# A gated attention and mixture-of-experts block on one core: ramp and attention order rebuilt, GpSimd's early splits done step by step, fewer float32 products in the FFN

## The chip, the cores and the metric
The kernel runs on 1 core of one Trainium2 chip. The metric is device time in microseconds (us) of one execution; lower is better. Engines are named as in the profile: PE is TensorE's matmuls, PEld its weight loads, DVE VectorE, ACT ScalarE, POOL GpSimd, SP the engine that issues the DMAs.

## The reference
Two batches of 256 tokens with 128 features, and 512 context rows each.

```
x = x + tanh(g_xattn) * (attention(layernorm(x), ctx) @ Wo + bo)     # 8 heads of 64; keys and values
                                                                    # from 512 context rows and 256 own rows
x = x + tanh(g_ffn) * ffn(layernorm(x))
ffn(x): logits = x @ gate_w + gate_b; top 2 of 8 experts, softmax over the two
        out = sum_e combine[e] * (gelu(x @ w1[e] + b1[e]) @ w2[e] + b2[e])   # all 8 experts are computed
        + gelu(x @ ws1 + bs1) @ ws2 + bs2                                    # shared expert
```

## The kernel before
**Precision.** Most products are computed from float16 pairs. A float32 operand is scaled and written as a high half (hi) and a low half (lo), and `three` runs hi*hi, hi*lo and lo*hi into the same PSUM bank: three matmuls for one product. The second products of the FFN named in `FULL32` (experts 0 to 8 of batch 0, and the last product, number 17) read float32 operands directly instead, from the loaded weights in `ring` and the gelu output in `hid`.

**Ramp.** `x` and the context are loaded, the rows of x are normalised (statistics on DVE, the power on POOL), both are transposed on PE and split into hi (ACT) and lo (DVE). The items in `PRE` (context transposes `tc`, x transposes `tx`, keys of pair 0, queries of pair 0) come first. `split_a` splits Wk2, Wk1 and Wq: ACT writes the hi half, DVE the lo half.

**Attention.** A pair is two heads of one batch; there are 8 pairs, and each is cut into 3 units of 256 keys, so 24 steps (units), numbered 0 to 23. In step i, PE computes the scores of unit i (`scores`), the weighted values of an earlier pair (`values`, one head in each of two of every three steps), a chunk of the row maxima of the pair after the current one (`max_chunk`), and the projections listed in `LATE[i]`. ACT takes the exponential (`exp_unit`, L640), writes its hi half (`make_hi`, L648) and evicts the projections (L629). POOL computes the lo half of the probabilities (`prob_lo`, L541), and may be at most 3 units behind, since `prob` has 3 buffers. DVE reduces the maxima (`part_max`, L821), evicts the lo halves of the projections (L803) and normalises a pair of heads (`normalise`, L850). Until unit `DOUBLE0` the scores have one PSUM buffer: the scores of unit i+1 start after the exponential of unit i.

**Tail of a batch.** `tail` transposes the output of attention (O0, O1), multiplies by Wo (WO, with a bias row as two more matmuls), adds to x, normalises again (X) and computes the gates (GATE, COMB, B2). `TAIL_STEP` gives the step of each.

**FFN.** Steps from `FFN0` = 24. Product k (0 to 17; 9 per batch) has its first matmuls at step 24+k, gelu on ACT in the same step (L711), its second matmuls two steps later and the addition to `acc` on DVE (L971) three steps later. For a product not in `FULL32` the gelu output is split: DVE and ACT write a half of hi each (L935, L719), POOL the lo half (L561). The expert weights are split once, during batch 0: the hi half by ACT (L723, L728) or POOL (`early_hi` L503, `late_hi` L530), the lo half by DVE (`expert_lo`, L925), for expert 0 by POOL (`early_lo`, L515).

The order on each engine is that of its loop over the steps, written out by hand: an engine that waits holds all that stands behind it.

Of the kernel before, what the change touches and what calls it, by code (L numbers as in the profile page):

```python
# [13 lines left out]
F32 = mybir.dt.float32  # L14
# [25 lines left out]
RING = 7  # L40
# [20 lines left out]
DOUBLE0 = 15  # L61
# [8 lines left out]
EARLY_HI_STEP = (14, 17, 20)  # L70
EARLY_LO_STEP = (16, 19, 22)
WO_STEP = 12

W1_STEP = {4: FFN0, 5: FFN0 + 1, 6: FFN0 + 3, 7: FFN0 + 5, 8: FFN0 + 6}
# [3 lines left out]
W1_LATE, W2_LATE, W2P_LATE = list(W1_STEP), list(W2_STEP), list(W2P_STEP)  # L78
# [25 lines left out]
def values_of(s):  # L104
# [7 lines left out]
PRE = [(("tc", 0), 0), (("tx", 0), 2), (("k", 0, 0), 4), (("q", 0), 6)]  # L112
LATE = {
# [20 lines left out]
WARM_START, WARM_LAYERNORM, WARM_MAX, WARM_STEP = 14, 9, 4, 12  # L134
# [55 lines left out]
FULL32 = [*range(NE), NF - 1]  # L190
# [27 lines left out]
def block_kernel(nc, x, ctx_in, g_xattn, g_ffn, Wq1, Wk1, Wv1, Wk2, Wv2, Wo, bo,  # L218
                 gate_w, gate_b, w1, b1, w2, b2, ws1, bs1, ws2, bs2, out):
    stack = ExitStack()  # L220
    with stack:
# [12 lines left out]
        wa = sb("wa", [P, 2, NW, 512], F16)  # L234
# [12 lines left out]
        oT = qo  # L247
# [21 lines left out]
        bo_row = sb("bo_row", [1, D], F32)  # L269
        unit_row = sb("unit_row", [1, P], F32)  # L270
# [1059 lines left out]
```

## Time and profile before

| | |
|---|---|
| median of 3 runs | 158.71 us (158.71 to 159.02) |
| profiled execution, its own time | 158.72 us |
| its span in the trace | 156.9 us |
| mean granted TensorE clock | 0.999 |

The span is what the trace shows from the first instruction to the last, so 1.8 us of the execution's time lie outside of it. The times inside the trace are from the span's start.

### The profile page before, as it was taken

The page shows a single profiled execution, that of the slowest core. Times are in us where ns is not written, and L with a number is a line of the kernel's source. Part 1 is how long each engine was busy: PE and PEld are TensorE (multiplying, and loading weights), DVE is VectorE, ACT ScalarE, POOL GpSimd, SP SyncE. Part 2 cuts the span into 40 slices and gives each one's busy share as a digit, 9 for nine tenths or more (in the row PEclk, how much of TensorE's full clock was granted, in tenths as well). Part 3 has the DMA queues.
Part 4 walks back from the last instruction along what each step waited for, and adds up shares of the span by engine and source line. Part 5 has one row for each costly group of instructions (what it writes and reads, how often), then busy time and mean ns, then how long its engine had stood idle before and what let it go on. Part 6 is the DMA issues. An engine that isn't in the chain of part 4 may idle for free.

```text
span 156.9 us, 4455 instructions
## 1 busy us (share of the span) xinstructions
PE 143.6 (92%) x1844; PEld 110.4 (70%) x1844; DVE 107.6 (69%) x204; ACT 116.6 (74%) x196; POOL 97.6 (62%) x84
## 2 busy tenths in 40 slices
PE   7969699999899998986989789999999999999992
PEld 4624354466466565755767579999999999989992
DVE  1679898977867787769786565426674677597731
ACT  3546789998887889997657989875458576978730
POOL 5504988596555676999698988400260079688730
PEclk9999999999999999999999999999999999999999
DMA  5589880000000000400000000054000000100001
GB/s 151 183 295 265 266 255 0 0 4 2 4 0 6 0 4 0 117 23 0 4 0 4 4 0 4 0 148 123 0 0 6 0 2 0 38 0 4 0 4 33
DMA packets 10112, 7.66 MB, mean 49 GB/s; under 512 B 1086, under 2 KB 8300, under 8 KB 10092
## 3 DMA queue, kind: packets, MB, share of 16 engines
q1 hardware_dynamic: 10092, 7.38, 15.7%
q8 instruction: 15, 0.25, 0.7%
q14 instruction: 5, 0.04, 0.1%
HBM read 7.11 MB, written 0.26 MB: 47 GB/s over the span
## 4 chain that ended last, share of the span: by engine, by line
PE 67%; DVE 14%; ACT 9%; issue 5%; DMA 2%; POOL 1%; DVEq 0%; ACTq 0%
PE banks L1286 11%; PE banks L1000 11%; PE banks L1002 10%; PE banks L1001 10%; DVE part L821 6%; ACT prob L640 4%; PE banks L1179 3%; PE banks L1181 3%; PE banks L1180 3%; PE banks L1129 2%; ACT v_hi L629 2%; DMA x_sb<-in_x_dram 2%; PE banks L1147 2%; ACT p_hi L648 2%; PE banks L1139 2%
## 5 line engine op out<-in xcount | busy, mean ns | idle before, releaser
L541 POOL TENSOR_TENSOR p_lo<-prob,p_hi 128x1024 f16<-128x1024 f32 x23 | 49.3, 2150 | 14.9 <-ACT p_hi L648 14.9
L711 ACT ACTIVATE prob<-banks,b1T 128x256 f32<-128x256 f32 x72 | 28.1, 474 | 11.1 <-PE banks L1002 11.1
L821 DVE TENSOR_REDUCE part<-banks 128x2 f32<-128x1024 f32 (+1 forms) x24 | 29.0, 1215 | 1.6 <-PE banks L1102 1.5
L640 ACT ACTIVATE prob<-banks 128x1024 f32<-128x1024 f32 x24 | 24.5, 1021 | 6.9 <-PE banks L1147 6.8
L648 ACT ACTIVATE p_hi<-prob 128x1024 f16<-128x1024 f32 x24 | 25.4, 1057 | 0.8
L1000 PE MATMUL banks<-x2h,wf 128*128 128x256 f16 x72 | 19.6, 273 | 0.0
L1286 PE MATMUL banks<-ring,prob 128*128 128x128 f32 x160 | 19.6, 276 | 0.0
L1002 PE MATMUL banks<-x2h,wf 128*128 128x256 f16 x72 | 19.6, 273 | 0.0
L1001 PE MATMUL banks<-x2h,wf 128*128 128x256 f16 x72 | 19.6, 272 | 0.0
L561 POOL TENSOR_TENSOR k_both<-prob,k_both 128x1024 f16<-128x1024 f32 x8 | 17.1, 2132 | 4.1 <-ACT k_both L719 3.0
L1179 PEld LDWEIGHTS banks<-v_hi,p_hi 128*128 128x128 f16 x192 | 17.4, 98 | 2.8 <-issue 2.7
L1179 PE MATMUL banks<-v_hi,p_hi 128*128 128x65 f16 x192 | 19.2, 195 | 0.0
L1180 PE MATMUL banks<-v_lo,p_hi 128*128 128x64 f16 x192 | 19.1, 193 | 0.0
L1181 PE MATMUL banks<-v_hi,p_lo 128*128 128x65 f16 x192 | 19.0, 194 | 0.0
L1286 PEld LDWEIGHTS banks<-ring,prob 128*128 128x128 f32 x160 | 18.7, 192 | 0.1
L1180 PEld LDWEIGHTS banks<-v_lo,p_hi 128*128 128x128 f16 x192 | 17.5, 98 | 0.0
L1181 PEld LDWEIGHTS banks<-v_hi,p_lo 128*128 128x128 f16 x192 | 17.6, 97 | 0.0
L925 DVE SCALAR_TENSOR_TENSOR wf<-ring,wf 128x512 f16<-128x512 f32 x16 | 15.6, 996 | 1.1 <-ACT wf L723 1.1
L935 DVE CAST k_both<-prob 128x512 f16<-128x512 f32 x8 | 10.3, 1283 | 5.6 <-ACT prob L711 5.6
L1000 PE MATMUL banks<-wf,k_both 128*128 128x128 f16 x64 | 11.1, 219 | 0.1
L1002 PE MATMUL banks<-wf,k_both 128*128 128x128 f16 x64 | 11.1, 219 | 0.0
L1001 PE MATMUL banks<-wf,k_both 128*128 128x128 f16 x64 | 11.1, 219 | 0.0
(158 smaller groups left out, 331.5 us busy)
## 6 DMA issues: line engine op xcount, KB each, us to landing
ring<-in_L_ffn_w_dram SPq DMA_DIRECT2D x16, 256.0 KB, 4.1
wf<-in_ctx_dram SPq DMA_DIRECT2D x2, 256.0 KB, 5.2
ring<-in_L_xattn_Wk_dram SPq DMA_DIRECT2D x2, 256.0 KB, 4.4
ring<-in_L_xattn_Wv_dram SPq DMA_DIRECT2D x2, 256.0 KB, 7.4
ring<-in_L_ffn_ws_dram SPq DMA_DIRECT2D x2, 256.0 KB, 6.8
x_sb<-in_x_dram SPq DMA_DIRECT2D x1, 256.0 KB, 2.9
ring<-in_L_xattn_Wq_dram SPq DMA_DIRECT2D x1, 256.0 KB, 4.6
ring<-in_L_xattn_Wo_dram SPq DMA_DIRECT2D x1, 256.0 KB, 8.0
```

The source lines that it names most:

```text
L541: nc.gpsimd.tensor_tensor(p_lo[:, u % RINGP, :, :].rearrange("p a n -> p (a n)"), prob[:, u % RINGE, :], p_hi[:, u % RINGP, :, :].rearrang ...
L640: nc.scalar.activation(prob[:, u % RINGE, :], units(u).rearrange("p a n -> p (a n)"), ACT.Exp, scale=DH ** -0.5 / S_SCORE).then_inc(exp_do ...
L648: nc.scalar.activation(p_hi[:, u % RINGP, :, :].rearrange("p a n -> p (a n)"), prob[:, u % RINGE, :], ACT.Copy).then_inc(ph_act, 1)
L711: nc.scalar.activation(hid[:, k % NHID, c * T1:(c + 1) * T1], span(2 * (k % 2), HC * T1)[:, c * T1:(c + 1) * T1], ACT.Gelu, bias=b1T[:, e ...
L821: nc.vector.tensor_reduce(dst, src, AX_X, ALU.max).then_inc(part_done, 1)
L1000: nc.tensor.matmul(dst, w[0], a[0], start=start, stop=False)
L1001: nc.tensor.matmul(dst, w[0], a[1], start=False, stop=False)
L1002: return nc.tensor.matmul(dst, w[1], a[0], start=False, stop=stop)
L1179: nc.tensor.matmul(o_ps[:, half, q, :], ph, vh, start=(t == 0), stop=False, skip_group_check=True)
L1180: nc.tensor.matmul(o_ps[:, half, q, 0:DH], ph, vl, start=False, stop=False, skip_group_check=True)
L1181: last = nc.tensor.matmul(o_ps[:, half, q, :], pl, vh, start=False, stop=(t == KT - 1), skip_group_check=True)
L1286: last = nc.tensor.matmul(banks[:, 4 + k % 2, q * D:(q + 1) * D], hid[:, k % NHID, at:at + P], ring_f(k % NE)[:, 1, cols], start=(c == 0), ...
```

## The change
1. **Ramp.** x is loaded in two halves. Only batch 0's rows are normalised, transposed and split in the ramp; batch 1's statistics are taken at step 4, its power at step 5 on POOL (six small operations, four of them new), its rows are written by ACT at step 5, and its transposes become an item at step 6. ACT and DVE split the three weights after both transposes. Keys and queries of pair 0 have their own semaphores: ACT evicts hi and a scaled float32 copy (`raw0`), DVE the queries' hi, POOL subtracts for the lo halves. `open_scores(0)` runs the first twelve matmuls of unit 0 ahead of its shift; `close_scores` adds the last four.
2. **Attention order.** Queries are computed per batch (`q0`, `q1`) instead of for both; `LATE` is spread anew, out to step 16; `DOUBLE0` goes from 15 to 18. In the ramp, the lo halves of pair 1's keys and queries stand ahead of pair 1's maxima on DVE, and at step 0 PE takes the items ahead of the chunk. Values are normalised one head at a time in one shared region of bank 6.
3. **GpSimd.** The splits of expert weights 0 to 3 run at steps 1, 3 and 5 (expert 0) and at the nine steps of `EARLY_STEP`: hi, scaled and lo all on POOL. DVE's three `expert_lo` for them are gone. W2 of experts 5, 6 and 7 is split wholly by POOL at steps 25, 26 and 27.
4. **Output projection.** Wo is no longer split: its product reads float32, without the bias matmuls; POOL adds tanh(g)*bo to x beforehand. The transposed attention output is one DVE copy instead of ACT hi and DVE lo.
5. **FFN.** `FULL32` loses products 4 to 7. Products 0 and 1 have their first matmuls together at step 24. The last product's second half is in bank 7 with its own semaphore. `RING` goes from 7 to 8.

```diff
-RING = 7
+RING = 8
-DOUBLE0 = 15
+DOUBLE0 = 18
-EARLY_HI_STEP = (14, 17, 20)
-EARLY_LO_STEP = (16, 19, 22)
-WO_STEP = 12
+EARLY_STEP = (6, 7, 9, 10, 12, 13, 15, 16, 17)
+POOL_W2 = (5, 6, 7)
+POOL_W2_STEP = (FFN0 + 1, FFN0 + 2, FFN0 + 3)
-W2_STEP = {1: FFN0 + 2, 2: FFN0 + 4, 3: FFN0 + 7, 4: FFN0 + 8}
-W2P_STEP = {5: FFN0 + 4, 6: FFN0 + 5, 7: FFN0 + 6, 8: FFN0 + 8}
+W2_STEP = {4: FFN0 + 2, 1: FFN0 + 6, 2: FFN0 + 7, 3: FFN0 + 8}
-TAIL_STEP = [dict(zip(TAIL_STAGES, (16, 17, 19, 22, 23, 28, 29))),
+TAIL_STEP = [dict(zip(TAIL_STAGES, (16, 17, 18, 21, 23, 28, 29))),
+NORM_STEP = [20, 31]
-PRE = [(("tc", 0), 0), (("tx", 0), 2), (("k", 0, 0), 4), (("q", 0), 6)]
+PRE = [(("tc", 0), 0), (("tx", 0), 2)]
+K0_BANK, Q0_BANK = 4, 7
 LATE = {
     -3: [(("k", 0, 1), 4)],
-    -2: [(("q", 1), 7)],
-    0: [(("k", 0, 2), 4), (("q", 2), 7)],
-    1: [(("v", 0, 0), 4), (("v", 0, 1), 5), (("v", 0, 2), 7)],
-    2: [(("v", 0, 3), 4), (("v", 0, 4), 5)],
-    3: [(("v", 0, 5), 7)],
-    4: [(("k", 0, 3), 4), (("q", 3), 7)],
+    -2: [(("q0", 1), 7)],
+    0: [(("k", 0, 2), 4), (("q0", 2), 7)],
+    1: [(("v", 0, 0), 4), (("v", 0, 1), 5)],
+    2: [(("v", 0, 2), 7), (("v", 0, 3), 4)],
+    3: [(("v", 0, 4), 5), (("v", 0, 5), 7)],
+    4: [(("k", 0, 3), 4), (("q0", 3), 7)],
     5: [(("tc", 1), 7)],
-    6: [(("k", 1, 0), 4)],
-    7: [(("v", 1, 0), 4), (("v", 1, 1), 5), (("v", 1, 2), 7)],
...
+    6: [(("tx", 1), 4), (("v", 1, 0), 7)],
+    7: [(("k", 1, 0), 4), (("q1", 0), 7)],
+    8: [(("q1", 2), 7)],
...
+    16: [(("k", 1, 3), 4)],
 }
-WARM_START, WARM_LAYERNORM, WARM_MAX, WARM_STEP = 14, 9, 4, 12
+WARM_START, WARM_LAYERNORM, WARM_KEYS, WARM_MAX, WARM_STEP = 14, 4, 8, 3, 8
-FULL32 = [*range(NE), NF - 1]
+FULL32 = [*range(POOL_W2[0] - 1), NE - 1, NF - 1]
-        o_ps = banks[:, 6, 0:2 * QT * (DH + 1)].rearrange("p (h q d) -> p h q d", h=2, q=QT)
+        o_ps = banks[:, 6, 0:QT * (DH + 1)].rearrange("p (q d) -> p q d", q=QT)
...
             for i in range(CHUNK0, STEPS):
+                if 0 < i < NU:
+                    open_scores(i)
                 if 0 <= i < NU:
-                    scores(i)
+                    close_scores(i)
...
```

New functions on POOL and ACT, with what they issue:

```
def second_by_pool(j):      # three 128x512 operations: hi = src*S_W; src = src*S_W; lo = src - hi
def add_bias():             # bo*tanh(g), then four 128x128 additions to x
def second_rows():          # ACT: two 128x128 rows of batch 1, scaled and shifted
```

## Rows read from the trace of the kernel before

**Rows 1.** The page's table of busy time: us, share of span, instructions.
```profile
PE 143.6 (92%) x1844; PEld 110.4 (70%) x1844; DVE 107.6 (69%) x204; ACT 116.6 (74%) x196; POOL 97.6 (62%) x84
```

**Rows 2.** The chain that ended last, in the ramp: start, us, what.
```profile
3.63 0.88 DVE stats L754 x4
...
6.29 1.22 DVE xn L772 x4
...
12.49 3.50 DVE part L821 x3
...
16.26 0.61 DVE qo L803
17.00 0.31 PE banks L1112
...
18.89 0.88 DVE k_both L803
```

**Rows 3.** Timeline of ACT: start, duration, of exponentials 0, 1, 6 and 23.
```profile
18.54 1.02 ACT L640 ACTIVATE prob<-banks 128x1024 f32<-128x1024 f32 x1 [1.10 <-PE banks L1147]
...
22.63 1.02 ACT L640 ACTIVATE prob<-banks 128x1024 f32<-128x1024 f32 x1 [0.33 <-PE banks L1147]
...
37.68 1.02 ACT L640 ACTIVATE prob<-banks 128x1024 f32<-128x1024 f32 x1 [0.35 <-PE banks L1147]
...
90.67 1.01 ACT L640 ACTIVATE prob<-banks 128x1024 f32<-128x1024 f32 x1
```

**Rows 4.** Windows: stretch, its us, busy PE, PEld, DVE, ACT, POOL, clock, DMA.
```profile
28.00:38.00 10.00, 9.69 (x139) 6.03 (x136) 8.62 (x12) 9.56 (x14) 7.47 (x4) 1.00 0.01 2
...
100.00:110.00 10.00, 10.00 (x98) 9.46 (x97) 4.93 (x11) 6.68 (x16) 0.00 (x0) 1.00 0.39 107
```

**Rows 5.** Groups of instructions: busy us, mean ns of one, idle before them.
```profile
L541 POOL TENSOR_TENSOR p_lo<-prob,p_hi 128x1024 f16<-128x1024 f32 x23 | 49.3, 2150 | 14.9 <-ACT p_hi L648 14.9
...
L925 DVE SCALAR_TENSOR_TENSOR wf<-ring,wf 128x512 f16<-128x512 f32 x16 | 15.6, 996 | 1.1 <-ACT wf L723 1.1
...
L935 DVE CAST k_both<-prob 128x512 f16<-128x512 f32 x8 | 10.3, 1283 | 5.6 <-ACT prob L711 5.6
...
L629 ACT ACTIVATE v_hi<-banks 128x512 f16<-128x512 f32 x12 | 6.5, 589 | 0.2 <-PE banks L1002 0.2
...
L530 POOL TENSOR_TENSOR wf<-ring,c_sw 128x512 f16<-128x512 f32 x4 | 4.1, 1039 | 0.0
```

**Rows 6.** Timeline of DVE around step 16: start, duration.
```profile
71.48 2.47 DVE L925 SCALAR_TENSOR_TENSOR wf<-ring,wf 128x512 f16<-128x512 f32 x1
...
100.23 0.68 DVE L925 SCALAR_TENSOR_TENSOR wf<-ring,wf 128x512 f16<-128x512 f32 x1
```

**Rows 7.** Timeline of PE: matmuls that it waited for.
```profile
74.61 0.66 PE L1190 MATMUL banks<-ident,o_sb 128*128 128x128 f32 x4 [1.28 <-DVE qo L855]
...
88.65 0.41 PE L1207 MATMUL banks<-ident,xn 128*128 128x128 f32 x2 [0.89 <-ACT xn L655]
...
91.81 0.39 PE L1212 MATMUL banks<-gw,x2T 128*128 128x8 f32 x2 [0.59 <-DVE x2h L855]
```

**Rows 8.** Timeline of PE in the FFN: starts of work, one after the other.
```profile
108.62 0.22 PE L1000 MATMUL banks<-wa,qo 128*128 128x128 f16 x1
...
110.99 0.28 PE L1000 MATMUL banks<-x2h,wf 128*128 128x256 f16 x1
...
112.31 1.95 PE L1286 MATMUL banks<-ring,prob 128*128 128x128 f32 x16
```

**Rows 9.** The same view, product 10's second matmuls and what follows.
```profile
134.87 0.22 PE L1000 MATMUL banks<-wf,k_both 128*128 128x128 f16 x1
...
136.21 0.38 PE L1218 MATMUL banks<-ident,comb 128*9 128x128 f32 x2
```

**Rows 10.** The chain that ended last, in the FFN and at the end.
```profile
122.73 1.79 PE banks L1286 x16
...
154.13 0.35 DVE acc L971
```

More of the change, by code:

```diff
@@ L404, in item_out @@
             kind = ITEMS[n][0]
-            return span(BANK[n], KEYS) if kind == "k" else banks[:, BANK[n], :]
+            if kind == "k":
+                return span(BANK[n], KEYS)
+            return banks[:, BANK[n], 0:T1] if kind in ("tx", "q0") else banks[:, BANK[n], :]
+        raw0 = prob[:, RINGE - 1, :]
+        k0_out = span(K0_BANK, KEYS)
+        q0_out = banks[:, Q0_BANK, 0:T1]
+        k0_rows = [k_nat[:, hl, 0, 0, :] for hl in range(2)]
+        q0_rows = [q_nat[:, hl, 0, 0, :] for hl in range(2)]
         block = stack.enter_context(nc.Block())
@@ L688, in _ @@
                     exp_unit(i)
+                for b in range(B):
+                    if i == NORM_STEP[b]:
+                        normal_rows(b)
+                if 0 <= i < NU:
                     make_hi(i)
+                if i == NORM1_STEP:
+                    second_rows()
                 for n in late_items(i):
@@ L1032, in item_of @@
                 if kind == "tx":
-                    keep_warm(WARM_LAYERNORM, 6)
-                    for t in range(NT):
-                        pe.wait_ge(xn_ready, t + 1)
-                        last = nc.tensor.transpose(dst[:, t * P:(t + 1) * P], xn[:, t, :], ident[:, :])
+                    b = item[1]
+                    if b == 0:
+                        keep_warm(WARM_LAYERNORM, 6)
+                    for t in range(QT):
+                        pe.wait_ge(xn_ready, QT * b + t + 1)
+                        last = nc.tensor.transpose(dst[:, t * P:(t + 1) * P], xn[:, QT * b + t, :], ident[:, :])
                 elif kind == "tc":
@@ L1112, in shift_row, with score_tiles, open_scores @@
                 nc.tensor.transpose(shift_ps_rows, nmax[:, p % 2, :], ident[:, :]).then_inc(shift_ps, 1)
-            def scores(u):
+            def score_tiles(u):
+                p, third = divmod(u, UPP)
+                return [(n, half, slice(n * T1, (n + 1) * T1),
+                         slice((KT2 * third + n) * P, (KT2 * third + n + 1) * P))
+                        for n in range(KT2) for half in range(2)]
+            def open_scores(u):
                 p, third = divmod(u, UPP)
@@ L1144, in scores @@
                     pe.wait_ge(shift_done, p + 1)
-                for n, half, cols, keys in tiles:
+                for n, half, cols, keys in score_tiles(u):
                     rows = slice(DH * half, DH * half + DH)
@@ L1225, in tail, with first_matmul @@
                 last.then_inc(misc_ps, 1)
+            def first_matmul(k):
+                b, e = k // NE, EORDER[k % NE]
+                if k == 0:
+                    pe.wait_ge(part_done, UPP * NPAIR)
+                if k == 1:
+                    pe.wait_ge(exp_done, NU)
+                if k >= 2:
+                    pe.wait_ge(gelu_done, HC * (k - 1))
+                if k == 0:
+                    pe.wait_ge(e_lo, 1)
+                elif k < EARLY:
+                    pe.wait_ge(e_lo, k + 1)
+                elif k < NE:
+                    pe.wait_ge(w1_lo, k - EARLY + 1)
+                if k % NE == 0:
+                    pe.wait_ge(misc_done, MISC[(TAIL_X, b)] + 1)
+                tok = slice(b * T1, (b + 1) * T1)
+                for c in range(HC):
+                    cols = slice(c * P, (c + 1) * P)
+                    last = three(span(2 * (k % 2), HC * T1)[:, c * T1:(c + 1) * T1],
+                                 (wf[:, 0, e, 0, cols], wf[:, 1, e, 0, cols]),
+                                 (x2h[:, 0, tok], x2h[:, 1, tok]))
+                    if c % 2 == 1:
+                        last.then_inc(h_ps, 1)
@@ L1285, in _ @@
                             if k in FULL32:
[L1286 removed]
+                                last = nc.tensor.matmul(banks[:, y_bank(k, q), q * D:(q + 1) * D],
                                                         hid[:, k % NHID, at:at + P], ring_f(k % NE)[:, 1, cols],
```

377 lines of the change are left out of this document (212 added, 165 removed), and 12 rows, old and new, of the table LATE.

## The prediction

> **What bounds the kernel now.** I read the page's busy table first, then the chain that ended last, then PE's timeline for the places where it waited, and last the windows and groups of the engines that could take PE's place. PE is busy for 92% of the span, far ahead of ACT, DVE and POOL [rows 1]. A busy PE is not a PE at its peak, so I asked in each stretch what the next piece of work waits for.
>
> The exponentials mark the stretches [rows 3]: the ramp ends at 18.54 us, step 1 starts at 22.63, step 6 at 37.68, step 23 at 90.67.
> - Ramp (0 to 18.5): a serial chain. DVE's statistics, its four row normalisations, three maxima in a row of 3.50 us, then a low half of the queries (0.61) that has to leave bank 6 before the transpose of the shift may start at 17.00 [rows 2].
> - Steps 1 to 5 (22.6 to 37.7): ACT. In 28 to 38 it is busy for 9.56 of 10 us [rows 4]. With one score buffer every step needs an exponential, its high half and that step's evictions on ACT.
> - Steps 6 to 23: PE, with holes where it waits for DVE or ACT: 1.28 and 0.89 us are two of them [rows 7].
> - FFN (from 92): PE alone. In 100 to 110 it is busy for all of 10 us, while POOL has nothing to do [rows 4]. There a matmul saved is time saved.
>
> **The change part by part.**
>
> *Ramp.* Two tiles instead of four in the statistics and the normalisation save half of 0.88 and half of 1.22 us [rows 2]: 1.05. The rest is order: x's low half, the first queries and their evictions have 256 columns instead of 512, and ACT's weight splits now stand behind x's eviction, so that part is given back. I take 1.9 us earlier for the first maximum (12.49 to 10.6); the bounds are 1.0 (the halved work alone, all reordering worth nothing) and 2.6. The three maxima, 3.50 us, stay. The low half of 0.61 us ahead of the shift's transpose goes, since no item uses bank 6 any more: 0.6. Twelve of unit 0's sixteen matmuls are done before the shift; they lie in the 1.54 us between the transpose at 17.00 and the exponential at 18.54 [rows 2, 3], of which I take 0.3. That puts the first exponential 2.8 us earlier, at 15.7. What could be late next is POOL: it must subtract 768 and 256 columns for the first low halves, priced by its 2.15 us for 1024 columns [rows 5], so 2.2 us, within the 3.5 us of maxima: hidden. The granted clock is 1.00 in all the windows shown [rows 4]; 37 instead of 39 warming matmuls should leave it so.
>
> From exponential 0 to 1 it is 4.09 us now [rows 3]. There the low halves of pair 1 wait behind a maximum (the chain has 0.88 us for the keys' at 18.89 [rows 2]) and PE's next projection waits for them. With the halves first, the maximum (about 1.2 us, a third of 3.50) comes later, and the chunk behind it. Both are needed before scores 1, so only the overlap with PE's 1.3 us of projections is won; I take 0.3. Bounds: 0.9 gained, 0.3 lost. Exponential 1: 3.1 us earlier.
>
> *Steps 1 to 5.* ACT stays the bound. It gets two row normalisations for batch 1 and loses half of two query evictions and has one value eviction moved out of step 1 and back into step 3. By 0.59 us for 512 columns [rows 5] this is about +0.3 us in 15.05. POOL gets the two 1024-column passes of expert 0 that lay in the ramp (4.0 at 2.15 each, a little less).
>
> *Steps 6 to 23.* DVE's `expert_lo` at 71.48 takes 2.47 us, where the same operation takes 0.68 at 100.23, with POOL idle [rows 4, 6]. Behind it in DVE's queue stands the low half of the attention output, and PE waits 1.28 us for that [rows 7]. The change takes this and its two like out of DVE's queue and makes the eviction one copy: 1.28 gone. Batch 0's second normalisation comes two steps earlier, which removes the 0.89 at 88.65 (the rows) [rows 7]. Wo's product took from 108.62 to 110.99 for batch 1 [rows 8], 2.37 us; as eight float32 matmuls it should cost what a second product does, 1.79 [rows 10]: 0.58 less, here once. Against this, PE gets the queries of batch 1, which lay in ACT's stretch: two items of six 256-column matmuls, at 12 such in 1.32 us [rows 8], so 1.3, and two transposes, 0.2. Sum: -1.28 - 0.89 - 0.58 + 1.5 = -1.25. The even spread of values and keys is worth nothing in this sum, because a step lasts as long as PE's work in it; it fills steps 14 to 16, which are short now. Bounds: -2.9 (the moved work falls into holes) and +2.0 (see POOL below).
>
> The Trainium skill, "SBUF — State Buffer", Who interferes with whom, says that a DVE instruction with two SBUF inputs and a GpSimd instruction that reads SBUF exclude each other for the whole instruction, and whichever started first holds the port. Here the trace agrees: 2.47 against 0.68 us on L925. The rule speaks against part of this change too: see the third rival.
>
> *POOL.* By step 17 it has extra: two expert 0 passes (4.0), batch 1's power (1.4, an estimate: no row shown has these small operations; bounded by 0 and by one pass of 2.15), three `scaled` and three `lo` at 1.04 each (6.2), less Wo's low half (1.0): about 10.6 us. Its idle time ahead of `prob_lo` is 14.9 us in all [rows 5]. It fits, with 4 us to spare, and `prob` lets POOL be up to three units behind. I take nothing for it.
>
> *FFN start.* PE waits 0.59 us for x's low half before the gates [rows 7]; with the transposes a step earlier this is hidden: -0.6. Bounds: 0 and 1.0.
>
> *FFN.* A float32 second product takes 1.79 us [rows 10], a split one 1.34 (134.87 to 136.21 [rows 9]): 0.45 less, for four products 1.8. Wo for batch 1: 0.58. At the end one of the two additions of 0.35 us [rows 10] runs beside PE's last half: 0.35. Sum: -2.7. The cover for what the splits cost elsewhere: POOL gets nine operations of 1.04 (9.4 us) at steps 25 to 27 and four low halves of 2.15; it is idle from 100 to 110 now [rows 4]. ACT gets four conversions of half a gelu output, 512 columns each, bounded by its 0.59 for an eviction of that size [rows 5]. DVE gets four casts (1.28 mean, 10.3 us in 8 [rows 5]), which it does now for batch 1 in the same rhythm. But in batch 0 it also has the weights' low halves, so I give 0.6 back. Bounds: 0 and 3.0 (all the gain of this part).
>
> **Sum.** -3.1 + 0.3 - 1.25 - 0.6 - 2.7 + 0.6 = -6.75 us. The profiled execution took 158.72 us (span 156.9), practically the median of 158.71. So 158.7 - 6.8 = 151.9 us.
>
> **The rivals.**
> 1. *POOL binds in attention.* For: at the new pace the first `prob_lo` starts near 18, and until step 17 POOL has 17 times 2.15 plus 14 us to do, some 51 us, where the steps give it about 54. If a few of its operations run late, as small ones do, each late one holds an exponential three units on. Against: three units of slack. Price: half of the 4 us to spare is missed and 2.5 us are added: 154.4. The waits of ACT would show `<-POOL p_lo` in steps 7 to 17.
> 2. *The ramp's gain isn't kept.* The ramp runs ahead, but steps 1 to 5 are ACT's and gain nothing, and step 0 to 1 gets longer because the chunk now stands behind the projections and behind two low halves and a maximum. Price: the step gets 1.5 us longer instead of 0.3 shorter: 153.7.
> 3. *DVE binds in batch 0's FFN.* Steps 29 to 33 give it a cast, two additions (0.7) and a weight's low half each. With POOL busy, casts take 1.28 in the mean and `expert_lo` up to 2.47 [rows 5, 6]: 4.4 us against PE's 2.65 to 3.1. Four steps at 1 us more than PE, less the 0.6 that I gave: 155.3. Against: the sixteen L925 have a mean of only 1.0, and casts hide well for batch 1. By the skill's rule named above, the wait ends with POOL's operation, so it should be at most one operation each time.
> 4. *Slower.* Values are normalised one head at a time in one region: the second head's matmuls must wait for DVE's normalisation of the first, which stands behind evictions and a shift. It happens once per pair, eight times. It decides if it costs over 0.9 us each time; at 1.0 us it adds 8 us: 159.9. For: DVE held PE for 1.28 us in such a manner [rows 7]. Against: a full step (about 3 us) lies between the two heads, and DVE loses three operations of up to 2.47.
> 5. *The parts do more than I give.* The moved queries fall into holes (-1.5) and the lock costs nothing (-0.6): 149.8.
>
> **How the numbers follow.** Chances: the forecast (150.5 to 153.3) 0.56, rival 1 0.10, rival 2 0.11, rival 3 0.08, rival 5 0.07, slower by rival 4 0.05, a gain eaten up to nothing by a mixture 0.03. The range reaches from rival 5 to rival 3: 149.7 to 155.4, leaving out less than 2 in 10. A measurement of this kernel tells about 0.2% (0.3 us) from no change, so: faster 0.92, same 0.02, slower 0.06.
>
> **What would show each step.** The first maximum near 10.6 and exponential 0 near 15.7 (ramp); exponential 1 near 19.5; exponential 6 near 34.9; exponential 23 near 86.6; no PE wait above 1 us in front of the transposes of the output; no PE wait in front of the gates, which now start 1.14 us behind exponential 23 (90.67 to 91.81); from there to the end about 2.7 us less. Split second products of 4 to 7 take 1.34 us each with no hole before them. It would be wrong if ACT waits for POOL's `p_lo`, if PE waits for DVE's normalisation before values, if DVE is over 90% busy in steps 28 to 33, or if the clock falls below 1.00 in the ramp.

## The result, and the profile after

The changed kernel takes 150.46 us (median of 6 runs, 149.81 to 151.60), the kernel before 158.71 us beside it. The ratio is 0.9486, with a 95% interval of 0.9447 to 0.9526. The forecast was 151.9 us. The profiled execution took 151.20 us with a span of 149.4 us; before it was 158.72 and 156.9 us, so the two spans differ by 7.5 us. The profiled execution is 0.7 us slower than the median, so the stretches below explain 7.5 us and not the 8.25 us between the medians. In the table of the experiments the slowest run of e7 (152.94 us) and that of e10 (151.09 us) were in a slower state, and the ratios leave them out.

The first view is again the page's busy table (us, share of the span, instructions), answering to [rows 1].

```profile
PE 141.4 (95%) x1862; PEld 110.2 (74%) x1862; DVE 105.4 (71%) x217; ACT 116.7 (78%) x199; POOL 120.4 (81%) x108
```

PE has only 2.2 us less to do, but the span is 7.5 us shorter: most of the gain is time in which PE waited. POOL has 23 us more to do. ACT's timeline gives the same four exponentials as [rows 3]: 0, 1, 6 and 23.

```profile
16.99 1.02 ACT L709 ACTIVATE prob<-banks 128x1024 f32<-128x1024 f32 x1 [0.46 <-PE banks L1254]
...
20.10 1.02 ACT L709 ACTIVATE prob<-banks 128x1024 f32<-128x1024 f32 x1
...
36.05 1.01 ACT L709 ACTIVATE prob<-banks 128x1024 f32<-128x1024 f32 x1
...
86.59 1.00 ACT L709 ACTIVATE prob<-banks 128x1024 f32<-128x1024 f32 x1
```

With the four of before they cut the 7.5 us into stretches:

| stretch | before | after | difference | forecast |
|---|---|---|---|---|
| start to exponential 0 | 18.54 | 16.99 | -1.55 | -2.8 |
| exponential 0 to 1 | 4.09 | 3.11 | -0.98 | -0.3 |
| 1 to 6 | 15.05 | 15.95 | +0.90 | +0.3 |
| 6 to 23 | 52.99 | 50.54 | -2.45 | -1.25 |
| 23 to the end of the span | 66.23 | 62.81 | -3.42 | -2.7 |
| sum | 156.9 | 149.4 | -7.50 | -6.75 |

The chain that ended last shows where this profiled ramp lost time (start, us, what; it answers to [rows 2]).

```profile
1.20 3.67 DMA wf<-in_ctx_dram
5.01 1.09 PE banks L1124 x4
...
8.35 1.91 DVE wa L851 x3
```

The chain no longer begins with x's landing and DVE's statistics but with the landing of context 0. The windows (stretch, us, then busy PE, PEld, DVE, ACT, POOL, clock, DMA) answer to [rows 4], with one more stretch in which POOL is full.

```profile
28.00:38.00 10.00, 9.38 (x148) 6.53 (x147) 8.83 (x19) 9.90 (x14) 9.02 (x9) 1.00 0.01 3
45.00:56.00 11.00, 11.00 (x193) 7.42 (x189) 8.39 (x15) 9.59 (x12) 11.00 (x7) 1.00 0.01 3
...
100.00:110.00 10.00, 10.00 (x90) 9.36 (x89) 8.11 (x19) 5.44 (x13) 8.87 (x10) 1.00 0.01 2
```

ACT still bounds steps 1 to 5 (9.90 of 10). In the FFN, POOL is now busy for 8.87 us of 10 where it had nothing to do, and PE has all of 10 as before. The groups (busy us, mean ns of one, idle before them) answer to [rows 5].

```profile
L586 POOL TENSOR_TENSOR p_lo<-prob,p_hi 128x1024 f16<-128x1024 f32 x23 | 48.9, 2134 | 1.1 <-ACT p_hi L717 1.0
...
L1013 DVE CAST k_both<-prob 128x512 f16<-128x512 f32 x12 | 13.0, 1081 | 5.6 <-ACT prob L784 5.6
...
L1003 DVE SCALAR_TENSOR_TENSOR wf<-ring,wf 128x512 f16<-128x512 f32 x9 | 9.7, 1077 | 0.4 <-ACT wf L801 0.3
```

POOL's idle time before the probabilities' low halves fell from 14.9 to 1.1 us, while DVE's casts got cheaper (1.08 instead of 1.28 us). PE's timeline, for the matmuls that [rows 7] showed waiting:

```profile
67.36 0.39 PE L1071 MATMUL banks<-cT,wa 128*128 128x512 f16 x1 [0.22 <-DVE v_lo L878]
...
85.72 0.61 PE L1316 MATMUL banks<-gw,x2T 128*128 128x8 f32 x4
86.18 0.27 PE L1071 MATMUL banks<-x2h,wf 128*128 128x256 f16 x1
...
90.81 0.20 PE L1286 MATMUL banks<-v_hi,p_hi 128*128 128x65 f16 x1 [0.59 <-DVE o_sb L928]
...
117.57 0.61 PE L1316 MATMUL banks<-gw,x2T 128*128 128x8 f32 x4 [0.15 <-DVE x2h L933]
```

The waits of 1.28, 0.89 and 0.59 us are gone. The gates start 0.87 us ahead of exponential 23 instead of 1.14 behind it. One new wait of 0.59 us is that of the values behind head 14's normalisation.

How full PE is from exponential 6 to the first FFN matmul is read from two more windows, the first of before (37.68 to 92.28), the second of after (36.05 to 86.18):

```profile
37.68:92.28 54.60, 49.10 (x832) 34.36 (x831) 40.27 (x60) 45.87 (x53) 43.24 (x26) 1.00 0.04 12
```
```profile
36.05:86.18 50.13, 49.79 (x833) 35.74 (x830) 36.92 (x72) 42.70 (x51) 48.45 (x32) 1.00 0.01 2
```

PE was idle for 5.50 us of this stretch and is idle for 0.34. The three waits of [rows 7] are 2.76 us of it. The other 2.7 us are four waits that neither [rows 7] nor the prediction has. Two of them, in PE's timeline of before (the wait for a maximum, `part`, comes again at 69.71 and 79.31):

```profile
42.14 0.39 PE L1000 MATMUL banks<-wa,cT 128*128 128x512 f16 x1 [0.69 <-DVE k_both L803]
...
61.57 0.39 PE L1102 MATMUL banks<-k_both,qo 64*128 64x256 f16 x4 [0.67 <-DVE part L821]
```

The same view for Wo's product and a split second product, answering to [rows 8] and [rows 9] (each lasts until the next start shown):

```profile
103.46 1.95 PE L1306 MATMUL banks<-wo,k_both 128*128 128x128 f32 x16
105.24 0.27 PE L1071 MATMUL banks<-x2h,wf 128*128 128x256 f16 x1
...
110.39 0.22 PE L1071 MATMUL banks<-wf,k_both 128*128 128x128 f16 x1
...
111.73 0.27 PE L1071 MATMUL banks<-x2h,wf 128*128 128x256 f16 x1
```

Wo takes 1.78 us, a split second product 1.34. And the end of the chain, answering to [rows 10]: one addition of 0.35 us behind PE's last matmul, not two.

```profile
145.20 1.85 PE banks L1406 x16
...
147.08 0.35 DVE acc L1050
```

### The profile page after: what moved, and what is told of

It is laid out like the page before. It is cut to its first block, busy times and chain, and to the rows that moved or that the text cites. A ratio compares the mean times of both kernels' runs of the same rounds, so it can differ in the third digit from the quotient of the medians.

```text
span 149.4 us, 4560 instructions
## 1 busy us (share of the span) xinstructions
PE 141.4 (95%) x1862; PEld 110.2 (74%) x1862; DVE 105.4 (71%) x217; ACT 116.7 (78%) x199; POOL 120.4 (81%) x108
## 4 chain that ended last, share of the span: by engine, by line
PE 70%; ACT 11%; POOL 6%; issue 4%; DVE 4%; DMA 2%; SPq 0%; POOLq 0%; ACTq 0%; DVEq 0%
PE banks L1071 11%; PE banks L1073 10%; PE banks L1072 10%; PE banks L1406 7%; PE banks L1286 4%; PE banks L1288 3%; PE banks L1287 3%; PE banks L1227 3%; POOL p_lo L586 3%; PE banks L1190 3%; PE banks L1306 3%; DMA wf<-in_ctx_dram 2%; PE banks L1254 2%; PE banks L1241 2%; PE banks L1234 2%
## 5 line engine op out<-in xcount | busy, mean ns | idle before, releaser
L621 POOL TENSOR_TENSOR k_both<-prob,k_both 128x1024 f16<-128x1024 f32 x12 | 25.6, 2131 | 7.5 <-ACT k_both L792 6.1
L1013 DVE CAST k_both<-prob 128x512 f16<-128x512 f32 x12 | 13.0, 1081 | 5.6 <-ACT prob L784 5.6
L1071 PE MATMUL banks<-wf,k_both 128*128 128x128 f16 x96 | 16.7, 219 | 0.1
L1073 PE MATMUL banks<-wf,k_both 128*128 128x128 f16 x96 | 16.7, 219 | 0.0
L1072 PE MATMUL banks<-wf,k_both 128*128 128x128 f16 x96 | 16.7, 219 | 0.0
L1406 PE MATMUL banks<-ring,prob 128*128 128x128 f32 x96 | 11.8, 276 | 0.0
L1406 PEld LDWEIGHTS banks<-ring,prob 128*128 128x128 f32 x96 | 11.2, 192 | 0.0
L1050 DVE SCALAR_TENSOR_TENSOR acc<-banks,comb_s,acc 128x128 f32<-128x128 f32 x26 | 7.9, 342 | 4.2 <-PE banks L1073 3.2
```

The lines of the kernel that those rows point to most:

```text
L621: nc.gpsimd.tensor_tensor(hid_lo[:, k % HB, :], hid[:, k % NHID, :], hid_hi[:, k % HB, :], ALU.subtract).then_inc(hl_done, 1)
L1071: nc.tensor.matmul(dst, w[0], a[0], start=start, stop=False)
L1072: nc.tensor.matmul(dst, w[0], a[1], start=False, stop=False)
L1073: return nc.tensor.matmul(dst, w[1], a[0], start=False, stop=stop)
L1406: last = nc.tensor.matmul(banks[:, y_bank(k, q), q * D:(q + 1) * D], hid[:, k % NHID, at:at + P], ring_f(k % NE)[:, 1, cols], start=(c == ...
```

## The experiments

All are the changed kernel with the edit given, except b1, which edits the kernel before. From e4 on, the base has e4's edit too. "Exp. 0" is the start of exponential 0, "0 to 23" the time from there to exponential 23, "23 to product" that from exponential 23 to the start of the last product's second matmuls, all in the profiled execution. The last one leaves out the last output DMA. The kernel before has 72.13 and 61.42 there.

| | median us (lowest to highest) | ratio to before, 95% | exp. 0 | 0 to 23 | 23 to product |
|---|---|---|---|---|---|
| after | 150.46 (149.81 to 151.60) | 0.9486 [0.9447, 0.9526] | 16.99 | 69.60 | 58.45 |
| e1 four products float32 | 151.98 (150.97 to 152.72) | 0.9563 [0.9512, 0.9613] | 15.97 | 69.60 | 59.69 |
| e2 DVE low halves back | 151.09 (150.32 to 151.90) | 0.9511 [0.9470, 0.9553] | 15.54 | 69.60 | 59.04 |
| e3 POOL lighter | 150.20 (149.67 to 151.64) | 0.9475 [0.9416, 0.9533] | 15.90 | 69.60 | 58.48 |
| e4 context by ScalarE | 150.02 (149.78 to 150.12) | 0.9441 [0.9427, 0.9455] | 15.87 | 69.60 | 58.49 |
| e5 values bunched | 150.97 (150.51 to 151.99) | 0.9510 [0.9474, 0.9547] | 15.90 | 70.29 | 58.46 |
| e6 pair normalised | 150.34 (150.16 to 151.85) | 0.9483 [0.9436, 0.9529] | 15.68 | 69.60 | 58.61 |
| e7 maxima first | 150.39 (150.30 to 152.94) | 0.9462 [0.9443, 0.9481] | 15.96 | 69.74 | 58.44 |
| e8 products 0, 1 apart | 149.72 (149.61 to 151.29) | 0.9450 [0.9411, 0.9488] | 15.73 | 69.59 | 58.18 |
| e9 Wk2's split first | 149.65 (149.08 to 149.79) | 0.9416 [0.9399, 0.9432] | 15.47 | 69.60 | 58.46 |
| e10 both | 149.41 (148.84 to 151.09) | 0.9393 [0.9377, 0.9408] | 15.51 | 69.61 | 58.18 |
| b1 before, POOL splits | 157.31 (157.05 to 157.41) | 0.9898 [0.9883, 0.9912] | 18.47 | 70.58 | 61.36 |

One kernel's runs differ by 2.0 us in e3, while the last two columns repeat to 0.02 and 0.05 us in the kernels that don't touch their stretch. So small effects are read from the stretches below, and only large ones from medians.

**e1: products 4 to 7 read float32 again.**

```diff
-FULL32 = [*range(POOL_W2[0] - 1), NE - 1, NF - 1]
+FULL32 = [*range(NE), NF - 1]
```

> Second products 4 to 7 in float32 again, everything else as in the changed kernel (5 to 7 wait for GpSimd's split weights, since it scales them in place). Theory A (TensorE is the bound in the FFN, a float32 second product costs 0.45 us more than a split one): 4 times 0.45, so 1.8 us more than the changed kernel's 150.5, 152.3. Rival (the split products pay their gain back in casts and waits on VectorE and GpSimd): no change within 0.5 us, 150.0 to 151.0.

Measured: exponential 23 to the end takes 149.6 - 85.57 = 64.03 us instead of 62.81: the four split products are worth 1.22 us (1.24 by the table's last column). PE's starts, grouped by kind of work (worked out from the timeline; start, us until the next kind):

```
            e1                          after
products 4  109.38 ring,prob  1.78      110.39 wf,k_both  1.34
         5  112.47 ring,prob  1.79      113.04 wf,k_both  1.34
         6  115.79 ring,prob  1.79      115.92 wf,k_both  1.65
gates       117.58 gw,x2T     0.36      117.57 gw,x2T     0.47
         7  119.25 ring,prob  1.78      119.35 wf,k_both  1.34
later       129.65 x2h,wf     1.31      129.30 x2h,wf     1.44
```

Theory A has the right price, 0.45 us per product, and 1.24 of the 1.8 us arrive. From 4 times 0.45 = 1.8, what comes off is 0.31 behind product 6, 0.11 in the gates and 0.13 later: 0.55. The profile names DVE's low half of the next block's input (x2h) for 0.15 of it (at 117.57); for the rest it names nothing.

**e2: DVE's three `expert_lo` back.** GpSimd makes the high halves at steps 14, 17 and 20, DVE the low ones at 16, 19 and 22, as before.

```diff
-                if i in EARLY_STEP:
+                if i in EARLY_HI_STEP:
+                    early_hi(EARLY_HI_STEP.index(i) + 1)
...
+                if i in EARLY_LO_STEP:
+                    expert_lo(j, slice(0, 1)).then_inc(ed_lo, 1)
```

> The early splits of experts 1 to 3 as before the change: GpSimd writes hi at steps 14, 17 and 20, VectorE the lo halves at 16, 19 and 22; the rest as changed. Theory A (VectorE's two-input operations wait for GpSimd and hold the transposed attention output behind them): three lo operations of 1.7 to 2.5 us come back on VectorE and about 1.3 us of waiting on TensorE with them: 151.8. Rival (GpSimd has become the bound of attention, so six operations of 1.0 us less on it are worth more than the waits): 148.5 to 149.8.

Measured: 0 to 23 is the same 69.60 us. DVE's timeline has the three operations:

```profile
67.09 0.68 DVE L1000 SCALAR_TENSOR_TENSOR wf<-ring,wf 128x512 f16<-128x512 f32 x1
...
77.84 0.68 DVE L1000 SCALAR_TENSOR_TENSOR wf<-ring,wf 128x512 f16<-128x512 f32 x1
...
84.12 2.27 DVE L1000 SCALAR_TENSOR_TENSOR wf<-ring,wf 128x512 f16<-128x512 f32 x1
```

Two take 0.68 us. The third starts inside one of GpSimd's three low halves in a row and takes 2.27. PE's timeline and, below, GpSimd's:

```profile
83.81 0.20 PE L1287 MATMUL banks<-v_hi,p_hi 128*128 128x65 f16 x1 [0.38 <-POOL p_lo L589]
...
89.93 0.20 PE L1287 MATMUL banks<-v_hi,p_hi 128*128 128x65 f16 x1 [1.07 <-DVE o_sb L925]
```
```profile
67.70 2.13 POOL L589 TENSOR_TENSOR p_lo<-prob,p_hi 128x1024 f16<-128x1024 f32 x1 [1.13 <-ACT p_hi L714]
...
81.62 6.76 POOL L589 TENSOR_TENSOR p_lo<-prob,p_hi 128x1024 f16<-128x1024 f32 x3
```

The wait of 0.38 us comes before the third operation starts, and PE is ahead of ACT there. The wait of 1.07 us was 0.59 in after: the third operation pushes back what stands behind it on DVE, up to the normalised output that PE waits for. Exponential 23 to the last product is 59.04 instead of 58.45 us: 0.59 us is lost, all behind step 23. That is about half of theory A's 1.3, and the rival (a gain) is out. The Trainium skill, "SBUF — State Buffer", Who interferes with whom, has a DVE instruction with two SBUF inputs and a GpSimd instruction that reads SBUF exclude each other. The trace agrees: 2.27 us where a GpSimd low half had started first, 0.68 where the operation falls into a gap (67.09) or beside small operations of GpSimd's (77.84).

**b1: the kernel before, with the early splits on GpSimd alone** (the nine steps of `EARLY_STEP`; DVE's three removed, nothing else changed).

```diff
-EARLY_HI_STEP = (14, 17, 20)
-EARLY_LO_STEP = (16, 19, 22)
+EARLY_STEP = (6, 7, 9, 10, 12, 13, 15, 16, 17)
```

> The kernel before, with one part of the change: the early splits of experts 1 to 3 are done wholly by GpSimd at the nine steps of the changed kernel, and VectorE's three lo operations (6.66 us there) are gone. Theory A (they held the attention output's low half, 1.28 us of waiting on TensorE, and the Wo step): 1.3 to 2.5 us less than before's 158.8, 156.3 to 157.5. Rival (GpSimd's six more operations of 1.04 to 1.16 us make its low halves of the probabilities late, or the waits move elsewhere): 158.3 to 160.

Measured: 157.31 us, a ratio of 0.9898, and 0 to 23 is 70.58 instead of 72.13 us: -1.55. Theory A (156.3 to 157.5) holds. ACT's timeline shows step 17's two exponentials:

```profile
71.64 1.02 ACT L640 ACTIVATE prob<-banks 128x1024 f32<-128x1024 f32 x1
74.86 1.03 ACT L640 ACTIVATE prob<-banks 128x1024 f32<-128x1024 f32 x1 [0.39 <-PE banks L1143]
```

The step lasts 3.22 us and lasted 4.58: 1.36 less. On DVE the low half of the attention output now comes soon behind the maxima, where the `expert_lo` of [rows 6] stood:

```profile
71.33 0.16 DVE L828 TENSOR_REDUCE nmax<-part 128x4 f32<-128x8 f32 x1
71.71 0.69 DVE L855 SCALAR_TENSOR_TENSOR qo<-banks,qo 128x512 f16<-128x512 f32 x1 [0.21 <-ACT qo L681]
```

The three waits of 0.67 us for a maximum, 0.89 for xn and 0.59 for the gates are still there in b1. So the same edit is worth 1.4 to 1.6 us in the old order and 0.6 in the new one: what such an operation costs depends on where it falls.

**e3: GpSimd with six operations less.** Experts 1 to 3 keep the high half of their first weight; `scaled` and `lo` are left out and the low half is zero.

```diff
-                    elif stage == 1:
-                        early_scaled(j + 1)
-                    else:
-                        early_lo(j + 1)
+                    elif stage == 2:
+                        nc.gpsimd.memset(c_unused[:, :], 0.0).then_inc(e_lo, 1)
```

> GpSimd's scaled and lo passes for experts 1 to 3 are left out; the lo halves of these weights are zero (that part of the product is missing). Six operations of 1.04 to 1.17 us fewer between steps 7 and 17. If GpSimd binds in attention: 2 to 4 us less than the changed kernel, 146.5 to 148.5. If it only looks full (each three units of slack suffice): within 0.5 us, 150.0 to 151.0.

Measured: the window of e3 for 45 to 56 us.

```profile
45.00:56.00 11.00, 11.00 (x179) 7.00 (x177) 8.36 (x16) 9.83 (x12) 9.55 (x7) 1.00 0.01 3
```

POOL goes from 11.00 to 9.55 of 11 us, and 0 to 23 stays 69.60. GpSimd is busy for all of this stretch in after and still isn't what the stretch waits for. In after, exponential 10 (49.05 us) has a wait of 0.39 us that the profile puts down to a `p_lo`; in e3 the same exponential waits 0.38 us for PE's scores, so that `p_lo` cost nothing.

**e4: context 0's load issued on ScalarE's queue.**

```diff
-            sp.dma_start(ctx_sb[0], ctx_d[0]).then_inc(ld_ctx[0], 16)
+            nc.scalar.dma_start(ctx_sb[0], ctx_d[0]).then_inc(ld_ctx[0], 16)
```

> Only the context load of batch 0 is issued from ScalarE's queue instead of second in SyncE's. In the changed kernel its landing (4.88 us) is the first link of the chain. Theory A: it is issued 0.5 us earlier and lands 0.4 us earlier, and the whole kernel ends 0.3 to 0.5 us earlier: 150.1. Rival (the x load, which now shares the engines with it, lands later and the chain moves there, or what the ramp gains is lost behind GpSimd by step 2): no change.

Measured: 149.78 to 150.12 us in four runs; after had 149.81 to 151.60. From DVE's first statistics to the first maximum it is 3.32 to 10.69 = 7.37 us here; in the profiled execution of after it was 2.93 to 11.80 = 8.87, in e1, e2 and e3, which have SP's load too, 7.87, 7.37 and 7.69. In the kernels on e4's base with the same ramp it is 7.36, 7.36, 7.61 and 7.36 (e5, e6, e7, e8). But the statistics start later there (3.14 to 3.36 us instead of 2.90 to 3.02), as the rival said, and exponential 0 comes no earlier than in e1 to e3 (15.68 to 15.96 and 15.54 to 15.97). What changes is the spread. Without the profiled execution, the runs of one kernel lie within 0.1 to 0.7 us in e4 to e10, the 152.94 of e7 apart, and within 1.1 to 2.0 us in after and e1 to e3. PE's first transposes of the context, in e4 and then in after:

```profile
4.16 0.63 PE L1125 MATMUL banks<-ident,wf 128*128 128x128 f32 x4
```
```profile
5.01 1.09 PE L1124 MATMUL banks<-ident,wf 128*128 128x128 f32 x4 [0.81 <-DMA wf<-in_ctx_dram]
```

**e5: the two spread value projections back in their neighbours' steps.**

```diff
-    11: [(("v", 1, 2), 7)],
-    12: [(("v", 1, 3), 7)],
+    11: [(("v", 1, 2), 7), (("v", 1, 3), 4)],
...
-    14: [(("v", 1, 4), 4)],
-    15: [(("v", 1, 5), 5)],
+    14: [(("v", 1, 4), 4), (("v", 1, 5), 5)],
```

> On the changed kernel with the context load issued from ScalarE (150.02 us). Only two value projections move: batch 1's tile 3 from step 12 to 11 and tile 5 from step 15 to 14, so that steps 12 and 15, whose chunk of maxima is the second of a pair, have no projection behind it, as before the change. Theory B (the projection behind the second chunk covers the maximum that the third chunk waits for; kernel before had three such waits of 0.67 us on TensorE): two waits of about 0.7 us come back, 151.2 to 151.6. Theory A (as predicted: the spread is worth nothing while TensorE is full): 149.9 to 150.2.

Measured: 0 to 23 is 70.29 instead of 69.60 us. ACT's timeline, exponentials 11 and 12 of e5:

```profile
50.68 1.02 ACT L708 ACTIVATE prob<-banks 128x1024 f32<-128x1024 f32 x1
...
54.27 1.02 ACT L708 ACTIVATE prob<-banks 128x1024 f32<-128x1024 f32 x1 [0.39 <-POOL p_lo L583]
```

Steps 11 to 16 last 3.59, 2.39, 3.06, 4.03, 2.40 and 3.41 us, 18.88 in all; spread they last 2.95, 3.25, 2.71, 3.03, 3.26 and 3.00, 18.20. The bunched steps grow by 0.64 and 1.00 us, the emptied ones behind them shrink by 0.86 each, and the next ones grow by 0.35 and 0.41. PE's timeline says why:

```profile
57.14 0.39 PE L1194 MATMUL banks<-k_both,qo 64*128 64x256 f16 x4 [0.53 <-DVE part L899]
...
66.63 0.39 PE L1194 MATMUL banks<-k_both,qo 64*128 64x256 f16 x4 [0.53 <-DVE part L899]
```

Two waits for a maximum are back, where e4 has none. The base has one wait of 0.22 us between exponential 6 and the FFN, which is gone here. Theory B has the right mechanism, at 0.53 us each instead of 0.7; theory A, the prediction's, falls.

**e6: a pair of heads normalised together,** in two regions of bank 6, as before.

```diff
-        o_ps = banks[:, 6, 0:QT * (DH + 1)].rearrange("p (q d) -> p q d", q=QT)
+        o_ps = banks[:, 6, 0:2 * QT * (DH + 1)].rearrange("p (h q d) -> p h q d", h=2, q=QT)
...
-                if values_of(i) is not None:
+                if values_of(i) is not None and values_of(i) % 2 == 1:
```

> Same base. Only the normalisation goes back to a pair of heads in one reciprocal and one multiply (o_ps with both heads). Theory A (one head at a time costs VectorE nothing that TensorE waits for): within 0.3 us of 150.0 in attention. Rival B (splitting it lets the multiply of the first head leave the queue ahead of the second chunk's maximum, which shortens the way to the third chunk): 0.2 us more at each of seven pairs, 151 to 151.5. The 0.59 us wait ahead of the fifteenth head's values should go, since two regions exist: 0.6 less in the FFN's first steps.

Measured: 0 to 23 is 69.60 us as with single heads: theory A holds, rival B falls. But the wait at the FFN's start, which was expected to go, stays: PE waits 0.74 us for the pair instead of 0.59 for the head, and 23 to product is 58.61 instead of 58.49 us:

```profile
89.65 0.20 PE L1288 MATMUL banks<-v_hi,p_hi 128*128 128x65 f16 x1 [0.74 <-DVE o_sb L930]
```

**e7: the second pair's maxima ahead of its low halves again,** on DVE at step -1, and the chunk ahead of the items on PE at step 0.

```diff
-                if i == -1:
-                    for n in items_at(i):
-                        item_of(n)
...
+                if i == -1:
+                    for n in items_at(i):
+                        item_of(n)
```

> Same base. VectorE takes pair 1's first maximum ahead of the low halves of its keys and queries, and TensorE the chunk ahead of the projections at step 0, as before the change. Prediction's step: 0.3 us more between exponentials 0 and 1 (3.1 to 3.4 us). Theory B (the gap is set wholly by this order, the kernel before had 4.09 us): 3.11 goes to about 4.0, and what comes back by step 2 (3.76 us now, held by the same queue) is half of it: 150.5 in all.

Measured: exponential 0 to 1 is 3.97 us instead of 3.11, exponential 1 to 2 is 3.04 instead of 3.76. Of 0.86 us won in the first step, 0.72 is given back in the second; 0 to 23 is 69.74, so the order is worth 0.14 us. Theory B has the first step right (about 4.0), and more than its half comes back. DVE's timeline of step 0, in e7 and then in after:

```profile
15.30 1.22 DVE L901 TENSOR_REDUCE part<-banks 128x2 f32<-128x1024 f32 x1
16.43 0.95 DVE L879 SCALAR_TENSOR_TENSOR k_both<-banks,k_both 128x768 f16<-128x768 f32 x1
```
```profile
16.33 0.95 DVE L878 SCALAR_TENSOR_TENSOR k_both<-banks,k_both 128x768 f16<-128x768 f32 x1
17.19 0.41 DVE L878 SCALAR_TENSOR_TENSOR qo<-banks,qo 128x256 f16<-128x256 f32 x1
17.52 1.22 DVE L900 TENSOR_REDUCE part<-banks 128x2 f32<-128x1024 f32 x1
```

**e8: products 0 and 1 not together.**

```diff
-                if k == 0:
-                    first_matmul(0)
-                    first_matmul(1)
-                elif 2 <= k < NF:
+                if 0 <= k < NF:
```

> The changed kernel with context 0's load issued on ScalarE's queue (as e4) in which the first matmuls of FFN products 0 and 1 are no longer issued together: product 1's stands one step later. Theory A (what ends the FFN's start is VectorE's normalised output of the last heads, and issuing the two products together only fills TensorE while it waits): apart, TensorE has one product's work less (about 1.3 us) ahead of the values' wait, the wait of 0.59 us before the values of the FFN's start grows by up to 1.3 us, and the time is 150.5 to 151.3. Theory B (TensorE is the bound there and its order is worth nothing): the wait goes or moves, exponential 23 to the end stays at 62.8, and the time is 150.0 within 0.3.

Measured: theory A falls, the wait doesn't grow. Theory B is the nearer one (149.72 us is in its range), but the order isn't worth nothing. The values' wait gets shorter, 0.38 instead of 0.59 us, and exponential 23 to the last product's matmuls is 58.18 instead of 58.49 us.

```profile
89.17 0.20 PE L1287 MATMUL banks<-v_hi,p_hi 128*128 128x65 f16 x1 [0.38 <-DVE o_sb L929]
```

So issuing the two together costs 0.3 us here, of which the wait is 0.2. Only this stretch shows it: e8's ratio overlaps that of e4. The profiled execution has a span of 149.5 us all the same, because its last output came late (the last product's start to the end is 6.0 us, in e4 4.3).

**e9: Wk2 split first** on ACT and DVE, between context 0's eviction and that of x.

```diff
-            for n in range(len(PRE)):
-                item_of(n)
-            for w in RAMP_SPLITS:
+            item_of(0)
+            split_a(WK2)
+            item_of(1)
+            for w in (WK1, WQ):
```

> The changed kernel with context 0's load issued on ScalarE's queue (as e4) and with one order changed in the ramp: key weight 2's high part (ScalarE) and low part (VectorE), which the first shift's product and the first pair's keys need, go ahead of the eviction and the low half of context 1's transposed x. Theory A (the ramp from the first maxima to the first exponential, 5.18 to 5.20 us in every run so far, is set by the chain of the split of key weight 2 through the keys to the shift): first exponential about 0.5 us after... i.e. at 15.4 instead of 15.87, span 147.9, time 149.5. Theory B (the chain goes through context 1's x, and the weight had slack): the first exponential stays at 15.9 or comes later by the delay of x's low half, about 0.5 us, and the time is 150.0 to 150.5. Either way first exponential to exponential 23 should stay 69.60.

Measured: the first exponential comes at 15.47 instead of 15.87 us. The gain isn't where theory A put it: first maximum to exponential 0 is 5.18 us as ever (10.29 to 15.47). It lies ahead of the first maximum: from DVE's first statistics it takes 7.08 instead of 7.37 us, and the statistics began 0.11 earlier. Theory A's 15.4 us is nearly met, its reason isn't. DVE's timeline of e9: one weight's low half now stands where DVE waited for x.

```profile
6.47 0.68 DVE L853 SCALAR_TENSOR_TENSOR wa<-ring,wa 128x512 f16<-128x512 f32 x1
7.07 0.42 DVE L880 SCALAR_TENSOR_TENSOR xT<-banks,xT 128x256 f16<-128x256 f32 x1
```

**e10: e8 and e9 together.**

> Both edits together: key weight 2's split first in the ramp, and the FFN's first two products apart. If each works by itself in its own stage the two differences to e4 add up: between 149.3 and 150.8 us. If the ramp's edit gains 0.5 and the FFN's edit is free it is 149.5.

Measured: 149.41 us, ratio 0.9393 [0.9377, 0.9408], which doesn't overlap the changed kernel's 0.9486 [0.9447, 0.9526]: about 1% faster than it, with e4's edit counted in. Against e4 (0.9441 [0.9427, 0.9455]) the two edits give 0.5%. The statistics to the first maximum take 6.98 us, 23 to the last product 58.18: both gains are there.

## Why the prediction was right or wrong

The time was right to 1.4 us (151.9 forecast, 150.46 measured, just below the band of 150.5 to 153.3 that had the chance of 0.56), and every stretch in sign. Part of that is luck. In the profiled execution the ramp and the FFN gained 1.25 and 0.7 us less than forecast, and what lies between exponential 6 and the first FFN matmul gained 2.6 us more.

The step that failed is the list of PE's waits in attention. The prediction took three (1.28, 0.89 and 0.59 us, [rows 7]) and gave the even spread of values and keys nothing, "because a step lasts as long as PE's work in it". The trace of before has four more waits, 2.7 us, and PE's idle time fell by 5.16 us.

- **Ramp (forecast -2.8, measured -1.55 in one execution).** The first maximum was to come at 10.6 and exponential 0 at 15.7. In the profiled execution they came at 11.80 and 16.99. In e1, e2 and e3, with the same loads and the same order, the first maximum came at 10.77, 10.35 and 10.71, exponential 0 at 15.97, 15.54 and 15.90: the forecast was about right for these. What my sum lacked is that context 0's landing can become the start of the chain once x is needed less. PE's first transposes stood at 5.01 us in after, at 4.32 in e2 and 4.57 in e3. The first maximum is 1.45 us later than in e2 and the transposes only 0.69, so the rest of that difference is open. The smaller spread of the runs from e4 on points at the load, but no run shows its landing and its time together for more than one execution. First maximum to exponential 0 was 6.05 us and is 5.19, 0.86 less. The forecast was 0.9 (the low half of 0.61 and 0.3 for the early matmuls); the two weren't measured apart.
- **Exponential 0 to 1 (-0.3; measured -0.98) and steps 1 to 5 (+0.3; measured +0.90).** I bounded the first at 0.9 and chose by the overlap with PE's projections. e7 measures the reordering alone: -0.86, then +0.72 one step later. So the two misses are mostly one: what the low halves gain in step 0 goes back in step 1. I hadn't followed the moved maximum into the next step. Net of both stretches: forecast 0.0, measured -0.08.
- **Steps 6 to 23 (-1.25; measured -2.45) and FFN start (-0.6; measured -2.0).** The exponentials are ACT's marks, and in after PE is ahead of ACT at the end. The last scores start 3.2 us before exponential 23, in before 1.7 us; the first FFN matmul comes 0.41 us before that exponential instead of 1.61 behind it. I had taken the gates' place behind exponential 23 as fixed. So the two stretches are read together, by PE: 54.60 us were 50.13, -4.47, where -1.85 was forecast. Of the forecast, -2.77 were waits and +0.92 was work (the queries' 1.5 less Wo's 0.58). Measured, the idle time is 5.16 us less and the work 0.69 us more. The work was sized about rightly; the waits were missed by 2.4 us.
- **Which edit ended which wait.** The 1.28 us was sized rightly: b1 gives 1.36 in its step, 1.55 in all. "The even spread of values and keys is worth nothing" is wrong: e5 brings back two of before's three waits for a maximum, and 0.69 us. A projection behind a pair's second chunk gives PE work while DVE reduces that maximum. The same projection in the neighbouring step doesn't, though the sum of PE's work is the same. The 0.69 us wait at 42.14, the 0.89 for xn and the 0.59 before the gates are gone in after; the edits that I hold responsible for them (the new banks and order in `LATE`, the earlier stages of the tail) weren't tried one by one, nor was `DOUBLE0`.
- **FFN (-2.7 + 0.6 = -2.1; measured -1.4).** From the first FFN matmul to the end of the span it was 64.62 us and is 63.22. Wo's 0.58 (2.37 to 1.78 us; it is sixteen float32 matmuls and not eight, at the price taken), the end's 0.35 and 0.45 for each split product hold; the four splits, 1.8 by themselves, come to 1.22 with what they push. The 0.6 given back was the right size (0.55 in e1), but not where I put it: not casts in batch 0, but the gap around the second batch's gates. What I missed is the 0.59 us wait of the values behind head 14: 1.22 + 0.58 + 0.35 - 0.59 = 1.56, of 1.40 measured. Part of that wait comes from issuing products 0 and 1 together, which I had priced at nothing and which costs 0.3 (e8).
- **Rival 1, POOL binds:** POOL was as full as the rival says, 11.00 of 11 us, and it didn't bind (e3). My count of its work had no term for the bias additions (16.37 to 18.71 us in POOL's timeline of after, 2.3 us); the power of batch 1 measured 1.4 in all, as estimated. That the slack of three units decides is argued: no run has fewer buffers. The sign that I named, a wait of ACT for a `p_lo`, shows up once in after (0.39 us, exponential 10) and twice in e5. The chain that ended last leads through POOL from 16.37 to 25.90 us, but no exponential waits for a `p_lo` there, and whether POOL holds steps 0 to 2 wasn't tried.
- **Rival 2, the ramp's gain isn't kept:** wrong in size. The step got 0.98 us shorter, and 0.9 was given back by exponential 6, most of it by the order itself (e7).
- **Rival 3, DVE binds in batch 0's FFN:** casts take 1.08, weight halves 1.08 us; DVE is busy for 8.11 of 10 us in 100 to 110. PE has no hole there. The one wait for DVE in this part is 0.15 us at 117.57.
- **Rival 4, head by head:** it costs nothing in attention (e6: 69.60 both ways), and the wait at the FFN's start isn't its doing (0.74 us with pairs). That the full step between the two heads covers it fits, but wasn't tried.
- **Rival 5, the parts do more:** the nearest of the rivals, 149.8, but not by its reason. Between exponential 6 and the FFN PE's work grew by 0.69 us (the queries less Wo), so the queries weren't free; what gave more was the waits.

## What to carry to other kernels

Follow a moved instruction through the next step as well: here 0.86 us won at one exponential came back as 0.72 at the next. List every wait of the engine that bounds a stretch, until they add up to its idle time in the window: here three of seven were priced, 2.76 of 5.50 us. Where work stands is not free either: bunching two projections cost 0.69 us with the same sum, because DVE's maximum was no longer covered. And an engine's busy share says little on its own: GpSimd at 100% of a stretch, with three buffers of slack, cost nothing, while one held DVE operation ahead of what PE needs cost 1.4 us in b1's place and nothing in two of e2's three.

## What was not expected of the hardware

- Nearly the whole spread between the profiled executions lies at the two ends. Exponential 0 to 23 takes 69.59 to 69.61 us in nine kernels (after, e1 to e4, e6, e8 to e10), but the first maximum came between 10.35 and 11.80 us in after and e1 to e8, and the last two output DMAs took 1.6 us to land (median) in after and e4 and 2.4 in e7. From the last product's start to the end of the span it is 4.3 to 4.4 us in after, e1 to e4 and e9, and 5.6 to 6.2 us in e5 to e8 and e10. The page's list of DMA issues for the last microseconds shows it (queue and line, KB each, median us to landing), for after and for e7:

```profile
out_dram<-acc SPq DMA_DIRECT2D x2, 64.0 KB, 1.6
```
```profile
out_dram<-acc SPq DMA_DIRECT2D x2, 64.0 KB, 2.4
```

- One and the same DVE operation (128x512, two inputs) took 0.68, 0.68 and 2.27 us in one execution (e2), by where GpSimd stood. GpSimd's operation that began while DVE's long one ran took 2.58 us, the two before it 2.1.
- GpSimd can be given 23 us more (97.6 to 120.4 us busy) without its own operations getting slower: 2.15 before, 2.13 us after for 1024 columns.
